# Output of a recurrent loop on one core: from 128-step tiles turned on TensorE to a 32x32 block transpose on VectorE in each of 128 equal turns

## The reference

```
scale = 1.0 / np.sqrt(np.float32(weight.shape[0]));  ys = y * scale
d = rsqrt(einsum('bi,io->bo', ys * ys, weight * weight) + EPS)
x = x + einsum('bsi,io->bso', x * ys[:, None, :], weight) * d[:, None, :]
xW = einsum('ntd,dk->tnk', x, Wx) + b           # h0 = y, c0 = 0
def step(carry, xw_t):
    a = xw_t + prev_h @ Wh                       # (2, 256) @ (256, 1024)
    i, f, o = sigmoid(a[:, :H]), sigmoid(a[:, H:2H]), sigmoid(a[:, 2H:3H]);  g = tanh(a[:, 3H:])
    next_c = f * prev_c + i * g
    next_h = o * tanh(next_c)
x = x + hs                                       # hs: the next_h of all 1024 steps
```

## Time and profile before

| | |
|---|---|
| median of three runs | 2111.53 us (2111.23 to 2111.78) |
| profiled execution, first to last instruction (span) | 2109.4 us |
| busy: PE, PEld | 1884.8 us (89%), 1744.9 us (83%) |
| busy: DVE, ACT, POOL | 1250.0 us (59%), 707.7 us (34%), 480.7 us (23%) |
| first and last cell scan (L617) | 92.4 us, 2104.3 us |

### The profile page before, as it was taken

How to read it: one execution, slowest core, us unless ns; L and a number is a source line. 1 busy time by engine, 2 the same in 40 slices (tenths; PEclk the granted TensorE clock), 3 DMA queues, 4 the chain that set the end, 5 groups by cost and what they waited for, 6 DMA issues and landing times. The chain is left out here.

```text
span 2109.4 us, 138886 instructions
## 1 busy us (share of the span) xinstructions
PE 1884.8 (89%) x57612; PEld 1744.9 (83%) x57612; DVE 1250.0 (59%) x8257; ACT 707.7 (34%) x5179; POOL 480.7 (23%) x1298
## 2 busy tenths in 40 slices
PE   8999999999989998899989999899998999989998
PEld 5588888888878888888878888788887888878887
DVE  3366666666656665566656666566665666656665
ACT  2233333333333333333333333333333333333333
POOL 1122222222222222222222222222222222222221
PEclk9855555555555555555555555555555555555555
DMA  2000000000000000000000000000000000000000
GB/s 85 2 0 0 0 0 7 0 0 0 0 8 0 0 0 1 7 0 0 0 1 7 0 0 0 7 1 0 0 0 8 0 0 0 0 8 0 0 0 5
DMA packets 5214, 7.67 MB, mean 4 GB/s; under 512 B 268, under 2 KB 4632, under 8 KB 5144
## 3 DMA queue, kind: packets, MB, share of 16 engines
q1 hardware_dynamic: 4872, 6.30, 0.9%
q10 hardware_dynamic: 272, 0.26, 0.0%
HBM read 4.46 MB, written 2.10 MB: 3 GB/s over the span
## 5 line engine op out<-in xcount | busy, mean ns | idle before, releaser
L302 PE MATMUL psum<-h_parts,wh_p 128*128 128x2 f16 (+1 forms) x45056 | 1370.9, 166 | 12.6 <-issue 12.4
L302 PEld LDWEIGHTS psum<-h_parts,wh_p 128*128 128x128 f16 x45056 | 1286.7, 104 | 28.9 <-issue 12.8
L302 PE MATMUL psum<-ring,ident_b 128*128 128x4 bf16 (+2 forms) x12288 | 492.6, 168 | 202.1 <-DVE psum L617 179.2
L302 PEld LDWEIGHTS psum<-ring,ident_b 128*128 128x128 bf16 x12288 | 409.7, 105 | 286.2 <-DVE psum L617 260.3
L692 ACT ACTIVATE sig_f<-psum 128x4 f32<-128x4 f32 x1024 | 178.0, 174 | 1136.3 <-DVE psum L608 1136.3
L234 POOL CAST ring<-xw 128x64 bf16 (+1 forms) x256 | 121.3, 474 | 1447.2 <-POOLq L272 1413.2
L608 DVE TENSOR_REDUCE psum<-psum 128x4 f32<-128x8 f32 x1024 | 179.2, 175 | 430.9 <-PE psum L302 430.9
L620 DVE SCALAR_TENSOR_TENSOR h_parts<-scan_h 128x4 f16<-128x4 f32 x1024 | 176.5, 172 | 248.4 <-ACT scan_h L701 248.4
L697 ACT ACTIVATE scan_h<-psum 128x2 f32<-128x2 f32 x1024 | 178.2, 174 | 134.3
L610 DVE TENSOR_REDUCE psum<-psum 128x4 f32<-128x8 f32 x1024 | 179.1, 175 | 52.4 <-PE psum L302 13.5
L623 DVE TENSOR_TENSOR_SCAN h_parts<-scan_h,h_parts 128x12 f16<-128x12 f32 x1024 | 187.5, 183 | 35.1
(11 more groups left out here) (81 smaller groups left out, 221.8 us busy)
## 6 DMA issues: line engine op xcount, KB each, us to landing
x_rows<-in_x_dram SPq DMA_DIRECT2D x4, 512.0 KB, 8.6
out_dram<-y_rows SPq DMA_DIRECT2D x7, 256.0 KB, 2.1
wh_sb<-in_L_cond_Wh_dram SPq DMA_DIRECT2D x1, 1024.0 KB, 6.0
wx_sb<-in_L_cond_Wx_dram SPq DMA_DIRECT2D x1, 1024.0 KB, 10.9
w_sb<-in_L_cond_weight_dram ACTq DMA_DIRECT2D x1, 256.0 KB, 2.8
out_dram<-y_rows SPq DMA_DIRECT2D x2, 128.0 KB, 1.7
small_rows<-in_cond_dram SPq DMA_DIRECT2D x1, 2.0 KB
small_rows<-in_L_cond_b_dram SPq DMA_DIRECT2D x1, 4.0 KB
```

What stands on the lines that cost most here:

```text
L302: return nc.tensor.matmul(out_, lhs, rhs, start=first, stop=last, skip_group_check=True)
```

## The change

All engines now run one loop of `NI` = 128 equal turns. `save` (POOL) no longer adds into `xt` but writes the sum of `xt` and `hring` to `y_cols`, 32 columns that hold one turn (2 sequences x 8 steps x 2 chunks of features). At step 4 of the next turn DVE turns `y_cols` by one 32x32 block transpose into `y_rows` (128 x 32), and SP stores the turn in four DMAs of 4 KB, one for each group of 32 partitions, whose places in `out` come from the turn's number. POOL waits for the transpose (`y_turned`) before the first `save` of a turn, DVE waits for the stores of the turn before (`s_out`) before its transpose. The turning on PE, the copies on ACT, `y_tile` and the three copies of the turn's code are gone; a last transpose and four stores stand behind the loop for the last turn. The core of the diff (declarations left out):

```diff
@@ -107,8 +107,8 @@
         scan_h = sb("scan_h", [P, CB, 3])
         h_parts = sb("h_parts", [P, 2, CB, 3], F16)
-        y_tile = sb("y_tile", [P, K * B, P])
-        y_rows = sb("y_rows", [P, B, D])
+        y_cols = sb("y_cols", [P, B, UNROLL, K])
+        y_rows = sb("y_rows", [P, QUAD])
         psum = ctx.enter_context(nc.psum_tensor("psum", [P, 8, BANK], F32))
         banks = [psum[:, i, :] for i in range(8)]
@@ -191,17 +189,17 @@
                                  x[b, n * BANK:(n + 1) * BANK].rearrange("(n p) d -> p n d", p=P)).then_inc(s_x[b][n], 16)
             sp.dma_start(wx_sb[:, :, :], wx.rearrange("(k p) o -> p k o", p=P)).then_inc(s_wx, 16)
-            def store(n):
-                sp.dma_start(out[:, n * P:(n + 1) * P, :].rearrange("b t d -> t b d"), y_rows[:, :, :]).then_inc(s_out, 16)
-            for n in range(NT - 1):
-                sp.wait_ge(y_read, B * K * (n + 1))
-                store(n)
-            for b in range(B):
-                sp.wait_ge(y_act, b + 1)
-                sp.wait_ge(y_dve, b + 1)
-                sp.dma_start(out[b, (NT - 1) * P:T, :], y_rows[:, b, :]).then_inc(s_out, 16)
-            sp.wait_ge(s_out, 16 * (1 + NT - 1 + B))
+            out_t = out.rearrange("b t (k q i) -> q b (t k) i", k=K, i=QUAD)
+            stores = P // QUAD
+            sp.sem_inc(s_out, 2 * 16 * stores)
+            with sp.Fori(0, NI) as i:
+                sp.wait_ge(y_turned, i + 2)
+                sp.sem_inc(store_seen, 1)
+                for q in range(stores):
+                    sp.dma_start(out_t[q, :, bass.ds(i * (UNROLL * K), UNROLL * K), :],
+                                 y_rows[q * QUAD:(q + 1) * QUAD, :]).then_inc(s_out, 16)
+            sp.wait_ge(s_out, 16 * stores * (NI + 2))
         @block.gpsimd
         def _(pool):
@@ -241,12 +238,13 @@
             def save(half, t0):
-                now = xt_t[:, :, bass.ds(t0, HALF)]
-                nc.gpsimd.tensor_tensor(now, now, hring[:, half * HALF:(half + 1) * HALF, :].rearrange("p s c -> p c s"),
+                columns = y_cols[:, :, half * HALF:(half + 1) * HALF, :].rearrange("p b s k -> p k b s")
+                now = xt[:, :, :, bass.ds(t0, HALF)]
+                nc.gpsimd.tensor_tensor(columns, now, hring[:, half * HALF:(half + 1) * HALF, :].rearrange("p s (k b) -> p k b s", b=B),
                                         ALU.add).then_inc(hring_saved, 1)
-            nc.gpsimd.memset(rest[:, 0, 0:1], 0.0).then_inc(hring_saved, 2)
+            nc.gpsimd.memset(y_cols[:, :, :, :], 0.0).then_inc(hring_saved, 2)
             pool.wait_ge(s_wx, 16)
             nc.gpsimd.tensor_scalar(wx_sb[:, :, GATE_G * D:G * D], wx_sb[:, :, GATE_G * D:G * D], 2.0, None, ALU.mult).then_inc(s_wx2, 1)
@@ -264,8 +262,7 @@
             for s, v in last_read("xw"):
                 pool.wait_ge(s, v)
-            def iteration(i):
+            with pool.Fori(0, NI - 1) as i:
                 t = i * UNROLL
                 for half in range(2):
                     pool.wait_ge(ring_used, 1)
@@ -273,21 +270,14 @@
                     split(half, t + UNROLL + half * HALF)
                     pool.wait_ge(h_all, t + (half + 1) * HALF)
                     pool.sem_inc(pool_seen, 1)
+                    if half == 0:
+                        pool.wait_ge(y_turned, i + 1)
+                        pool.sem_inc(pool_seen, 1)
                     save(half, t + half * HALF)
-            pool.sem_inc(y_turned, 1)
-            with pool.Fori(0, NT - 1) as n:
-                with pool.Fori(0, TI) as i:
-                    iteration(pool.snap(n * TI + i))
-                pool.wait_ge(hring_saved, n * (2 * TI) + (2 * TI + 2))
-                pool.sem_inc(pool_seen, 1)
-                pool.wait_ge(y_turned, n * (B * K) + 1)
-                pool.sem_inc(pool_seen, 1)
-                nc.gpsimd.tensor_copy(y_tile[:, :, :], xt_t[:, :, bass.ds(n * P, P)]).then_inc(y_whole, 1)
-            with pool.Fori((NT - 1) * TI, T // UNROLL - 1) as i:
-                iteration(i)
             for half in range(2):
                 pool.wait_ge(h_all, T - UNROLL + (half + 1) * HALF)
+                if half == 0:
+                    pool.wait_ge(y_turned, NI)
                 save(half, T - UNROLL + half * HALF)
         @block.tensor
@@ -427,11 +417,9 @@
             for gate_mm in (f_mm, g_mm, o0_mm, o_mm):
                 pe.sem_inc(gate_mm, 1)
-            def iteration(i, n=None):
+            with pe.Fori(0, NI) as i:
                 t = i * UNROLL
                 for u in range(UNROLL):
-                    part = u - TILE_STEP
                     if u % HALF == 0:
                         pe.wait_ge(ring_full, 2 * i + u // HALF + 1)
                     pe.wait_ge(c_done, t + u + 1)
@@ -447,35 +435,11 @@
                     products(GATE_I, I_BANK, 0, 0, K)
                     pe.wait_ge(h_lo, t + u + 1)
                     products_apart(GATE_F, 0, K).then_inc(f_mm, 1)
-                    if n is not None and 0 < part <= B * K:
-                        pe.wait_ge(y_read, n * (B * K) + (part - B * K))
                     products_apart(GATE_G, 0, K).then_inc(g_mm, 1)
                     products(GATE_I, I_BANK, 1, 0, K).then_inc(ig_in, 1)
                     products_apart(GATE_O, 0, 1).then_inc(o0_mm, 1)
                     products(GATE_O, O_REST, 0, 1, K)
                     products(GATE_O, O_REST, 1, 1, K).then_inc(o_mm, 1)
-                    if n is not None and 0 <= part < B * K:
-                        b, k = divmod(part, K)
-                        if part == 0:
-                            pe.wait_ge(y_whole, n)
-                        pe.wait_ge(cell_in, (t + u + 1) * 2)
-                        nc.tensor.transpose(turned, y_tile[:, k * B + b, :], ident[:, :]).then_inc(y_turned, 1)
-            with pe.Fori(0, TI) as i:
-                iteration(i)
-            with pe.Fori(1, NT) as n:
-                iteration(pe.snap(n * TI), n)
-                with pe.Fori(1, TI) as i:
-                    iteration(pe.snap(n * TI + i))
-            pe.wait_ge(hring_saved, 2 + T // HALF)
-            for b in range(B):
-                for k in range(K):
-                    last = nc.tensor.transpose(banks[B * b + k][:, 0:P], xt[:, k, b, T - P:T], ident[:, :])
-                last.then_inc(y_filled, 1)
         @block.vector
         def _(dve):
@@ -625,12 +591,15 @@
                     if u % HALF == 0:
                         dve.wait_ge(hring_saved, 2 * i + u // HALF + 1)
                     nc.vector.tensor_tensor(hring[:, u, :], scan_h[:, :, 1], scan_h[:, :, 2], ALU.mult).then_inc(h_all, 1)
-            dve.wait_ge(s_out, 16 * NT)
-            for b in range(B):
-                dve.wait_ge(y_filled, b + 1)
-                nc.vector.tensor_copy(y_rows[:, b, 0:P], banks[B * b][:, 0:P]).then_inc(y_dve, 1)
+                    if u == HALF:
+                        dve.wait_ge(s_out, (i + 1) * (16 * (P // QUAD)))
+                        nc.vector.transpose(y_rows[:, :], columns).then_inc(y_turned, 1)
+            dve.wait_ge(hring_saved, 2 + 2 * NI)
+            dve.wait_ge(s_out, 16 * (P // QUAD) * (NI + 1))
+            nc.vector.transpose(y_rows[:, :], columns).then_inc(y_turned, 1)
         @block.scalar
         def _(act):
@@ -679,13 +648,9 @@
             act.sem_inc(f_act, 1)
             act.sem_inc(t_done, 1)
-            act.sem_inc(s_out, 16)
-            def iteration(i, n=None):
+            with act.Fori(0, NI) as i:
                 t = i * UNROLL
                 for u in range(UNROLL):
-                    part = u - TILE_STEP
                     step = act.snap(t + u + 2)
                     both = act.snap((t + u + 1) * 2)
                     act.wait_ge(f_sum, step)
@@ -699,25 +664,6 @@
                     nc.scalar.activation(scan_h[:, B:CB, 1], banks[O_REST][:, B:CB], ACT.Sigmoid, scale=unscale).then_inc(o_act, 1)
                     act.wait_ge(c_done, step)
                     nc.scalar.activation(scan_h[:, :, 2], cell[:, :, 2], ACT.Tanh).then_inc(t_done, 1)
-                    if n is not None and 0 <= part < B * K:
-                        b, k = divmod(part, K)
-                        if part == 0:
-                            act.wait_ge(s_out, n * 16)
-                        act.wait_ge(y_turned, n * (B * K) + (part + 2 - B * K))
-                        nc.scalar.copy(y_rows[:, b, k * P:(k + 1) * P], turned).then_inc(y_read, 1)
-            with act.Fori(0, TI) as i:
-                iteration(i)
-            with act.Fori(1, NT) as n:
-                iteration(act.snap(n * TI), n)
-                with act.Fori(1, TI) as i:
-                    iteration(act.snap(n * TI + i))
-            act.wait_ge(s_out, 16 * NT)
-            for b in range(B):
-                act.wait_ge(y_filled, b + 1)
-                nc.scalar.copy(y_rows[:, b, P:D], banks[B * b + 1][:, 0:P]).then_inc(y_act, 1)
 # ---- launch: one core; inputs and outputs as the reference has them ----
...
```

(14 more changed lines are left out.)

## The result

The changed kernel takes **2079.28 us** (median of four runs, 2078.44 to 2079.52) against 2111.66 us in runs beside it: ratio 0.9846, 95% interval 0.9832 to 0.9860, 1.5% faster. The prediction was 2078 us, with a range of 2076 to 2094.

A forecast was written before the change was run, and what follows sets the result against it. The step chain bounds the kernel, interrupted by 33.8 us, mostly PE's code fetches at tile boundaries. Span terms 92.4 + 1978.1 + 5.1 + 0.2 = 2075.8 us, plus 2.1 above the span, gave 2078 us; range 2076 to 2094.

The forecast's parts named there:

- (1): PE's loops: one copy of the turn ends code fetches at six boundaries, and the turning matmuls go; -33.8 us.
- E: Stalls are no fetches of extra code copies but come every 128 steps for another reason; 2111 us, chance 0.03.
- D: PE fetches code at each turn's branch back, 127 times some 5.3 us; 2751 us, chance 0.01.
- (2): DVE's block transpose, 128 times: 0.22 us each, hidden in 0.35 us left before L608 is due; 0 us.
- rival B: DVE's transpose hangs over its cover by 0.1 to 0.25 us a turn; +13 to +32 us, chance 0.12.
- (3): DVE's wait for the stores of the turn before: they land within a turn of 15.5 us; 0 us.
- (4): POOL's first save waits for the transpose, about 1.9 us later, done 3.5 us before it is wanted; 0 us.
- (6): End of the kernel: last save, transpose and four stores instead of turning and two stores; +0.2 us, bounds -0.3 and +1.5.
- A: The stalls go and all else is covered; 2078 us, own range 2076.5 to 2081, chance 0.80.

The follow-up runs named there:

- e1: Changed kernel with PE's turn again in three copies in nested loops, without turning matmuls; 2111.01 us, ratio 1.0003 to the kernel before.
- e2: Changed kernel with ACT's and DVE's turn in three copies in nested loops, PE's in one; 2078.72 us, ratio 0.9849 to the kernel before.
- e6: Changed kernel with three more block transposes per turn on DVE, into tiles nobody reads; 2079.18 us, ratio 0.9855 to the kernel before.
- e9: Changed kernel with seven more block transposes per turn on DVE; 2115.08 us, ratio 1.0026 to the kernel before.
- e10: Changed kernel with 30 stores per turn, of 4 or 6 rows of 128 bytes each; 2095.73 us, ratio 0.9936 to the kernel before.
- e7: Changed kernel with eight stores of 2 KB per turn in place of four of 4 KB; 2079.40 us, ratio 0.9858 to the kernel before.
- e8: Changed kernel with the last turn's four stores outside SP's loop, two on SP and two on ACT; 2077.90 us, ratio 0.9852 to the kernel before.
- e3: Changed kernel with PE's loop running 64 times over two copies of the turn; 2340.71 us.
- e4: Changed kernel with PE's loop running 32 times over four copies of the turn; 2201.14 us.

## Why the prediction was right

**(1) The fetches.** Forecast -33.8 us in the loop, measured 2011.9 - 1977.8 = 34.1. The reason is shown from both sides: the excess goes when PE holds one turn (5 packets), and 31.8 us of it come back when only PE's loops are put back (e1, 66 packets). The other 2.3 us are the turning and the first boundary, for which the forecast had 1.8 by subtraction. One count of the prediction is wrong: a turn has 448 matmuls and 448 weight loads, not 896 of each, and the expectation of e2 has twice the instructions too. The argument did not use it, but a reader who sizes a loop by it would be off by two. E, the rival in which the stalls have another cause, fell with e1, and D (a fetch at each turn) with the scans at 1.9333 us.

**(2) The transpose.** Forecast 0.22 us, measured 0.211. Forecast start 0.2 us behind L627's counterpart, measured 0.13. Forecast cover 0.35 us; what is left idle is 0.21 us. The sum held. That 0.22 met 0.211 so closely is in part luck: the forecast counts the 32 columns twice, which no run tests, and behind another transpose the same operation has a duration of 0.17 us (e6). The picture of rival B was too dark in one term: I took the whole duration as time in which DVE is taken, and e6 shows 0.1 us for each one that has nothing to wait for. The claim that a delay of L608 goes one for one into the step was nearly right, 0.36 us late made 0.31 us (e9), but the path was wrong: L610 has 0.17 us of room behind L608, and the delay went through ACT's sigmoid of f.

**(3), (4) The new waits.** Both cost 0, as forecast: no interval of the 1023 is above 1.94 us. An issue came every 0.83 us, which the bound in (3) held (0.37 and up to 0.5 for registers); four take 3.3 us of 15.5, and thirty were hidden too (e10).

**(6) The end** is the term that was off: forecast +0.2 us, with a bound of +1.5, measured +1.3. The step of it that failed is "then three more issues" at 0.45 us, taken from stores of 128 rows of 1 KB. It was 0.83 us, so three are 1.1 us more. A store of 2 x 16 pieces of 128 bytes took 0.63 us to issue, and one of 16 pieces 0.315 us (e7); the up to 0.15 us for address registers was right (0.14, e8).

**Sum.** Span 2075.8 forecast, 2076.7 measured: start +0.1, loop -0.3, end +1.1. The rest of the 1.3 us between 2078 and 2079.3 is the step from the profiled span to the median. What lies outside the span is 1.7 to 1.8 us in each of the four runs, not 2.1; but the profiled execution was the fastest of them (2078.44 us), and the others had spans of 2077.3 to 2077.7 us.

**The range and the chances.** The working of rival B does not agree with itself: an overhang of 0.1 to 0.25 us a turn, +13 to +32 us, gives 2091 to 2110 us, and not 2084 to 2098 for its lower half. The range up to 2094 held about a sixth of B, not two thirds, so its chance should have been some 0.82 and not 0.87. The result fell within A, so nothing hung on it.

## What to carry to other kernels

Where an engine "waits for issue" every so many turns and nowhere else, count the packets of the instruction queue and look at what the engine branches back over: a special first turn inside an outer loop cost PE two stalls each time round although it held hardly any work, and doing the special work a little in every turn, on an engine with a gap, can be cheaper than its sum of busy time says. Unrolling PE's loop from one turn to two made it 261 us slower, so count the instructions of a loop's body before it is made longer: 908 were held here and 1814 were not. And an addition to an idle gap on DVE is to be measured by the distance of starts, not by durations: four transposes, each of 0.21 us when it stands alone, fitted where 0.41 us had been idle.

## What the runs showed of the hardware that I had not expected

- A loop of PE whose body is 908 instructions branches back for nothing. With two or four times as many (e3, e4) each branch back stalls it for 4.1 or 3.9 us net, while the straight code between the branches, up to four turns, is fetched in time.
- Independent block transposes of 128 x 32 float32 on DVE take 0.21 us alone and start about 0.1 us apart in a row (e6, e9).
- The issue time of a store on SP depends on its shape: 0.37 us for 128 rows by 2 pieces of 1 KB, 0.63 us for 2 x 16 pieces of 128 bytes, 0.315 us for 16 such, 0.25 us for 4 (e10).
